# The second product of the feed-forward in float32r parts, and new orders of work in three kinds of attention block

## The reference

```python
x = layernorm(x + differential_attention(x))        # 16 heads, causal, two softmaxes per head
x = layernorm(x + ffn(x))

def _layer(x, ...):                                 # ffn() applies it twice (DEPTH = 2)
    h = shift_token(x)                              # second half of the channels one token later
    q, k, v = split(h @ wqkv, 3)                    # 8 heads of 64
    q, k = rotary_xpos(l2norm(q) * qs, l2norm(k) * ksc)
    x = x + local_attention(q, k, v) @ wo           # window 128, own and previous window
    h = layernorm(shift_token(x)) * lg + lb
    a, g = split(h @ w1 + b1, 2)                    # HID = 682
    x = x + (a * gelu(g)) @ w2 + b2
    return x
```

## Time and profile before

| | |
|---|---|
| median of 3 runs | 5556.42 us (5554.65 to 5564.04) |
| the profiled execution | 5557.89 us, span of its instructions 5555.8 us |
| granted TensorE clock over the span | 0.991 of full speed |
| busy: TensorE, VectorE, ScalarE, GpSimd | 95%, 75%, 63%, 23% |

### The profile page before, as it was taken

One profiled execution on the slowest core, in us unless ns is written; L12 is line 12 of the kernel. 1 busy time (PEld: TensorE's weight loads), 2 busy tenths in 40 slices (PEclk: granted clock), 3 DMA queues, 4 the chain that ended last, 5 costly groups with the idle time before them and its releaser, 6 DMA issues.

```text
span 5555.8 us, 150327 instructions
## 1 busy us (share of the span) xinstructions
PE 5271.0 (95%) x59592; PEld 2996.7 (54%) x59592; DVE 4168.2 (75%) x10819; ACT 3509.1 (63%) x7119; POOL 1259.2 (23%) x2489
## 2 busy tenths in 40 slices
PE   8999999999999999999789999999999999999997
PEld 3444444444444444544356666666666666666664
DVE  6888878888887888878567777777776777777774
ACT  4676667666666766767556566565565656656664
POOL 2222222222222222222212112111122121221211
PEclk9999999999999999999899999999999999999999
DMA  3333333233333333323110000000000000000000
GB/s 71 56 56 66 54 62 61 50 71 56 64 55 54 69 54 69 54 50 68 44 43 12 16 9 16 16 9 16 16 26 26 20 16 20 24 16 20 16 20 20
DMA packets 128829, 216.97 MB, mean 39 GB/s; under 512 B 40064, under 2 KB 40192, under 8 KB 127360
## 3 DMA queue, kind: packets, MB, share of 16 engines
q1 hardware_dynamic: 128128, 207.35, 18.4%
HBM read 46.78 MB, written 25.17 MB: 13 GB/s over the span
## 4 chain that ended last, share of the span: by engine, by line
PE 64%; ACT 15%; DVE 10%; issue 7%; POOL 4%; DMA 0%; POOLq 0%; ACTq 0%; SPq 0%; DVEq 0%
PE ps L617 23%; PE ps L746 14%; PE ps L1108 6%; PE ps L869 4%; ACT pt L1327 3%; PE ps L970 3%; PE ps L951 3%; PE ps L943 2%; ACT sm L1461 2%; DVE sm L1922 2%; ACT gates L1559 1%; PE ps L1049 1%; PE ps L1045 1%; PE ps L1046 1%; PE ps L927 1%
## 5 line engine op out<-in xcount | busy, mean ns | idle before, releaser
L1327 ACT ACTIVATE pt<-ps 128x1024 f32<-128x1024 f32 (+7 forms) x2048 | 1237.4, 654 | 620.1 <-PE ps L617 464.4
L746 PE MATMUL ps<-pt,va 128*32 128x512 f32 (+3 forms) x3072 | 1226.3, 487 | 22.3 <-POOL pt L2224 22.2
L746 PE MATMUL ps<-pt,ones 128*32 128x512 f32 (+3 forms) x6144 | 1236.3, 488 | 0.0
L746 PE MATMUL ps<-pt,vs 128*32 128x512 f32 (+3 forms) x3072 | 1230.0, 488 | 0.0
L1748 DVE CUSTOM_DVE_ANT_0 junk<-ps,causal 128x128 bf16<-128x128 f32 (+3 forms) x2048 | 978.1, 488 | 307.5 <-PE ps L617 291.7
L617 PE MATMUL ps<-kt,qt 96*32 96x512 bf16 (+3 forms) x12288 | 1017.4, 328 | 35.5 <-DVE mc L1748 16.3
L2224 POOL TENSOR_SCALAR_AFFINE_SELECT pt<-pt 128x256 f32<-128x256 f32 x1024 | 465.8, 455 | 1937.8 <-ACT pt L1327 1936.3
L617 PE MATMUL ps<-qt,kt 98*32 98x512 bf16 (+3 forms) x12288 | 836.6, 328 | 22.8 <-ACT pt L1327 22.0
L1752 DVE TENSOR_REDUCE mc<-ps 128x1 f32<-128x512 f32 x1024 | 706.4, 690 | 155.2 <-PE ps L617 124.5
L617 PEld LDWEIGHTS ps<-kt,qt 96*32 96x32 bf16 x12288 | 335.7, 94 | 578.4 <-DVE mc L1752 224.8
L1461 ACT ACTIVATE sm<-sm,mxw 128x256 f32<-128x256 f32 (+1 forms) x1024 | 494.0, 486 | 150.1 <-DVE mxw L1922 149.7
(11 more groups left out here) (170 smaller groups left out, 10221.6 us busy)
## 6 DMA issues: line engine op xcount, KB each, us to landing
qt<-part SPq DMA_DIRECT2D x768, 64.0 KB, 2.4
kt<-part SPq DMA_DIRECT2D x768, 64.0 KB, 2.5
ya<-wy SPq DMA_DIRECT2D x128, 128.0 KB, 2.3
yb<-wy SPq DMA_DIRECT2D x128, 128.0 KB, 2.3
xs<-between_phases SPq DMA_DIRECT2D x32, 512.0 KB, 3.8
xt<-in_x SPq DMA_DIRECT2D x16, 512.0 KB, 6.2
between_phases<-z SPq DMA_DIRECT2D x16, 512.0 KB, 2.8
between_phases<-xo SPq DMA_DIRECT2D x16, 512.0 KB, 2.7
```

What stands on the lines that cost most here:

```text
L746: mmi = pe.matmul(ps[32 * q:32 * q + 32, 4 + half, lo - half * 512:hi - half * 512], w, probs(kb)[:, i, lo - first(kb):hi - first(kb)], st ...
L1327: act.activation(probs(kb)[:, i, kb * P - first(kb):1024 - first(kb)], ps[:, 2 * i:2 * i + 2, :].rearrange("p a q -> p (a q)")[:, kb * P:1 ...
```

## The change

It does seven things, all in the second phase.

1. ffn_out is made in float32r parts: w2 is split once a layer into w2h (ScalarE) and w2l (GpSimd, in the place of w2) at the end of the block W % 64 = 5; the gated product is written over the gates, copied to hhh (inner_high, ScalarE) and the rest subtracted to hhl (inner_low, GpSimd, in the place of the gates). Each float32 matmul becomes three float32r ones, and the first half of the outputs waits for hhl row block by row block.
2. TensorE, c = 0 and c = 3: keys(W + 1) goes ahead of transpose_p(W, 0), and the other transposes stand elsewhere among the products.
3. TensorE, c = 2: scores(W, 2) and (W, 3) go ahead of transpose_p(W, 0), transpose_p(W, 2) and (W, 3) in among the hidden products, weigh behind all of them.
4. ScalarE, c = 2: exps(W, 2), exps(W, 3) and place_p(W, 1) go ahead of the Gelu table and the Gelus; place_p(W, 2) and (W, 3) follow the Gelus, and inner_high(m, 0) to (m, 4) stand in the rest of the block. In c = 0 and c = 3 squares(W + 1) goes ahead, exps(W, 2) and (W, 3) back; inner_high(m, 5) stands in c = 3.
5. VectorE: norms and rotations go forward between the normalises in c = 0 and c = 3; in c = 2 normalise(W, 2) and (W, 3) go between the gated products; final_add goes behind residual, final_normalise behind the gated products.
6. GpSimd: split_x(W + 2) becomes the first step of each block, with a third buffer of xh and xl; sum_channels goes ahead of final_channels; inner_low is added in c = 2 (behind VectorE's combine) and c = 3.
7. gate_out's first step waits for w2_full, since the gates' place is in use until the second product has been made.

```diff
-        xh = sb("xh", [P, 2, 2, P], F32R)
+        xh = sb("xh", [P, 3, 2, P], F32R)
@@ TensorE, ffn_out
-                    pe.wait_ge(w2_ready, sent(m // (2 * nb) + 1))
-                    pe.wait_ge(hh_done, done(m * HB + 6))
+                    pe.wait_ge(w2l_done, done(m // (2 * nb) + 1))
+                    pe.wait_ge(hh_done, done(m * HB + 5))
...
-                    mmi = pe.matmul(ps[:, fbank(m, 19 + oc), :], w2[rows, j, oc * P:(oc + 1) * P], hh[rows, j, :],
-                                    start=j == 0, stop=j == HB - 1)
+                    if oc == 0:
+                        pe.wait_ge(hhl_done, done(m * HB + j + 1))
+                    pe.matmul(out, w2h[rows, j, cols], hhh[rows, j, :], start=j == 0, stop=False)
+                    pe.matmul(out, w2l[rows, j, cols], hhh[rows, j, :], start=False, stop=False)
+                    mmi = pe.matmul(out, w2h[rows, j, cols], hhl[rows, j, :], start=False, stop=j == HB - 1)
@@ TensorE, c == 0 (c == 3 the same)
-                    transpose_p(W, 0)
                     keys(W + 1, 0)
                     keys(W + 1, 1)
+                    transpose_p(W, 0)
                     values(W, 0)
@@ TensorE, c == 2
                     keys(W + 1, 1)
+                    scores(W, 2)
+                    scores(W, 3)
                     final_variance(m - 1, W)
                     transpose_p(W, 0)
                     values(W, 0)
                     values(W, 1)
                     transpose_p(W, 1)
-                    scores(W, 2)
-                    scores(W, 3)
...
+                    hidden(m, 0, True)
+                    hidden(m, 1, True)
+                    hidden(m, 2, True)
                     transpose_p(W, 2)
+                    hidden(m, 3, True)
+                    transpose_p(W, 3)
+                    hidden(m, 4, True)
+                    transpose_q(W + 1)
                     weigh(W, 0)
@@ ScalarE
+            def inner_high(m, j):
...
+                act.wait_ge(hh_done, done(m * HB + j + 1))
+                act.activation(hhh[rows, j, :], gb_[rows, j, :], ACT.Copy).then_inc(hhh_done, 1)
@@ ScalarE, c == 2
                     values(W)
+                    exps(W, 2)
+                    exps(W, 3)
+                    place_p(W, 1)
                     inverse_norms(W + 1)
                     gelu_table(m)
                     gelu(m, 0)
...
                     gelu(m, 5)
-                    exp_table(m)
-                    exps(W, 2)
-                    exps(W, 3)
-                    place_p(W, 1)
                     place_p(W, 2)
                     place_p(W, 3)
+                    exp_table(m)
+                    inner_high(m, 0)
                     place_q(W + 1)
                     place_k(W + 1)
                     heads_high(W)
+                    inner_high(m, 1)
+                    inner_high(m, 2)
+                    inner_high(m, 3)
+                    inner_high(m, 4)
@@ VectorE, c == 3
                     normalise(W, 0)
+                    largest(W, 2)
+                    largest(W, 3)
                     normalise(W, 1)
-                    largest(W, 2)
-                    normalise(W, 2)
-                    largest(W, 3)
                     norms(W + 1)
                     rotate_own(W + 1)
+                    normalise(W, 2)
+                    rotate_other(W + 1)
                     normalise(W, 3)
-                    rotate_other(W + 1)
@@ GpSimd
+            def inner_low(m, j):
...
+                pool.wait_ge(hhh_done, done(m * HB + j + 1))
+                pool.tensor_tensor(hhl[rows, j, :], gb_[rows, j, :], hhh[rows, j, :], ALU.subtract).then_inc(hhl_done, 1)
...
+                split_x(W + 2)
+                if W % 4 == 3:
+                    inner_low(m, 5)
...
+                if m >= 0 and W % 4 == 2:
+                    pool.wait_ge(rot_done, done(W + 2))
+                    for j in range(5):
+                        inner_low(m, j)
```

More of the change, by code:

```diff
@@ L1226, in attend @@
                     ffn_out(m, 0, (2,), True)
-                    transpose_p(W, 1)
+                    transpose_p(W, 2)
                     ffn_out(m, 0, (3,), True)
@@ L1645, in attend @@
                     exps(W, 1)
+                    inner_high(m, 5)
+                    squares(W + 1)
+                    place_p(W, 0)
                     exps(W, 2)
-                    place_p(W, 0)
-                    squares(W + 1)
                     inverse_norms(W + 1)
@@ L1681, in _ @@
             exp_table(m)
+            for j in range(HB):
+                inner_high(m, j)
             final_squares(m)
@@ L2009, in gated @@
                     return
-                if j == 0:
-                    dve.wait_ge(w2_full, done(2 * m))
                 dve.wait_ge(ge_done, done(m * HB + j + 1))
@@ L2042, in attend @@
                     largest(W, 3)
-                    final_add(m - 1)
                     normalise(W, 1)
+                    norms(W + 1)
+                    rotate_own(W + 1)
                     normalise(W, 2)
+                    rotate_other(W + 1)
                     normalise(W, 3)
@@ L2048, in attend @@
                         add_bias(W // (nb * WIN))
-                    norms(W + 1)
-                    rotate_own(W + 1)
-                    rotate_other(W + 1)
                     combine(W + 1)
@@ L2054, in attend @@
                     residual(m, 1)
+                    final_add(m - 1)
                     centre(m)
@@ L2324, in _ @@
                 if m >= 0 and W % 4 == 0:
+                    sum_channels(m)
                     final_channels(m - 1)
-                    sum_channels(m)
                     sum_squares(m)
```

92 lines of the change are left out of this document (51 added, 41 removed).

## The result

The changed kernel takes 5617.35 us (median; 5616.74 to 5622.14) against 5555.53 us for the kernel before in the same comparison (5553.00 to 5564.04): a ratio of 1.011, 95% interval 1.0093 to 1.0128. It is slower by 62 us. The profiled execution has a span of 5615.0 us (before 5555.8) and a mean granted clock of 0.982 (before 0.991).

The account below looks back on a forecast made before the run. TensorE, busy 95% of the span, was taken to set the pace by its own order of work; -5 (c = 3) + 34 (c = 2) + 10 (c = 0) + 5 (once each) + 15 (clock) = +59 on 5557.9, so 5615 us, range 5545 to 5668.

Parts of the forecast that it names:

- c = 0: Blocks of kind 0: +1 us from the new order, +9 us from final_add meeting sum_channels in layer 2.
- c = 3: Second-product blocks: 22.59 us to 22.4, -0.15 a block, -5 us over 31 blocks, ends -25 and +34.
- c = 2: Gelu blocks: the later Gelu chain makes 21.54 us into 22.6, +1.1 a block, +34 us in all (+19 to +50).
- the wait on gated: Sign: in c = 2, hidden's first pass waits for VectorE's gated product about 3 us a block instead of 0.4.
- normalise above 0.69: Sign of meetings on the shared port: VectorE's normalise should take longer than 0.69 us, or GpSimd's subtractions longer than 1.3.
- subtractions above 1.3: Sign of meetings on the shared port: GpSimd's subtractions should take over 1.3 us, or VectorE's normalise over 0.69.
- the granted clock of 0.5: Sign: the clock's 1.2 GHz level should show behind TensorE's stalls in c = 2.
- once-each work: Splitting w2 twice and the tail, where the parts are made with nothing beside them: +5 us together, 0 to +12.
- the clock: Lower clock level behind most c = 2 stalls: +0.5 us a block, +15 us in all, ends 0 and +34.
- rival 1: c = 3 gives its full saving, -65 us; ends at 5541, deciding if c = 3 falls below about 20.9; chance 0.13.
- my price without meetings, 21.7: c = 3 block length without port meetings: 21.7 us, with waits of 0.3 and 0.9 back at two transposes.
- best case of 20.5: c = 3 block at best: 22.59 us falls to 20.5, with 1.75 saved on passes and about 0.34 wait hidden.

Follow-up runs that it names:

- e1: Changed kernel with the c = 2 blocks back in their old order on TensorE, ScalarE and VectorE: 5566.4 us, 1.001 of the kernel before.
- e10: e9 with w2l split in six pieces and layer 2's final_add at its old place in halves with short c = 0 blocks: 5482.9 us.
- e3: Changed kernel with GpSimd's six subtractions per half cut to 16 of 512 columns, TensorE's passes kept: 5573.1 us, 1.002 of the kernel before.
- e6: e5 with the second product's copies and subtractions moved to where VectorE needs no two SBUF inputs: 5508.9 us, 0.9908 of the kernel before.
- e8: Kernel before with only the new c = 0 and c = 3 orders and sum_channels ahead of final_channels, float32 product kept: 5546.5 us, ratio 0.9978.
- e9: e6 with layer 2's final variance between hidden 1 and 2 on TensorE, and final_inverse later on ScalarE: 5494.4 us, 0.9875 of the kernel before.
- e2: Changed kernel without ScalarE's two table loads in c = 2, a plain copy in place of the Gelu: 5539.0 us, 0.996 of the kernel before.
- e5: Changed kernel with ScalarE's c = 2 order altered: exps 2 ahead of values, place_p 1 behind the second Gelu: 5569.6 us, 1.002 of the kernel before.
- e7: e6 with w2l made in six pieces and final_add ahead of normalise 1 in the halves with long c = 0 blocks: 5508.3 us, ratio 0.9909.
- e4: Changed kernel with inner_high 1 to 4 moved into c = 3 and GpSimd's next-layer weight split ahead of inner_low: 5610.4 us, ratio 1.0085.

## Why the prediction was right, and which of its steps were off

The forecast (5615 on the profiled execution's 5557.9) and the measured 5617 agree, and the mechanism that it put first carries the loss: e1 gives 54 of the second phase's 60 us back by c = 2's order alone. Of the signs it named, the wait on gated (0.4 to 3.0 us), normalise above 0.69, subtractions above 1.3 (four took 5.47 us) and the granted clock of 0.5 are all there. The terms, though, agree less well than their sum: that it came within 2 us is luck, as c = 0 and the once-each work miss by 16 and 15 us in opposite directions, and c = 2 and the clock by 18 and 14. Two of the bounds do not follow from the prediction's own figures: the lower end of c = 3 is 31 x 0.89 = 28 us and not 25, and the range starts at 5545, above the 5541 of rival 1 that it says it reaches.

| term | predicted | measured |
|---|---|---|
| c = 2 without the clock, 31 blocks | +34 (19 to 50) | +15.6 in 29 steady blocks |
| the clock | +15 (0 to 34) | +29.1, 19 drops |
| c = 0 | +10 | -6.2 |
| c = 3 | -5 (-25 to +34) | 0 in steady blocks |
| once each | +5 (0 to 12) | +20 |

**c = 2.** The start was right: Gelu at 12.1 said, 11.92 measured; hidden 2 behind it at 13.38 (13.6 said), which is 0.2 of the difference. The end was summed too long: I had combine end at 19.5 and transpose_q wait 0.6 us for it, but normalise with its reciprocal and gated follow one another every 1.46 us, not 1.67, combine ends at 18.64, and transpose_q comes at 18.69 with hardly a wait. So a block with the clock up is +0.48 us in layer 1 and +0.60 in layer 2, not +1.1; the sum, 15.6, is below my lower bound of 19. The bounds varied ScalarE's chain alone; VectorE's, summed from single durations, was the one that was off.

**The clock.** The wait was foreseen, as was that not each one brings the lower level. The price of one was too low: I let part of the 1.6 us be hidden by the wait for combine, which did not exist; each drop costs 1.5 us, in 8 of 15 steady blocks of layer 1 (12.1 us) and 11 of 14 of layer 2 (17.0 us). Two errors that both came, in part, from that 0.6 us wait cancelled within c = 2: +44.7 us against +49.

**c = 0.** The step that failed is the sign. I feared norms' wait for squares in the short blocks (+0.5; measured -0.03) and gave the long ones -0.3 (measured -0.64). That final_add would cost the 7 short blocks of layer 2 by meeting sum_channels was right in kind (+0.54, said +1.3 on top of +0.5), and e10 takes it back; that it would take back the gain of the long ones was wrong (-0.63). The meeting is there in both kinds (sum_channels takes 2.17 us in W = 72 and in W = 76, 1.27 before), but TensorE reaches the mean later in a long block and waits only 0.31 us for it, against 1.18 in a short one.

**c = 3.** 22.61 measured, 22.4 said. The full first meeting (0.94 us, 0.8 said) and the one at the scaling behind the norms are there. But my price without meetings, 21.7, was wrong: e3 has 21.00 and e6 20.76. I had taken ScalarE's copies ahead of the exps as a cost of about 1.0 us (2.3 less 1.48 gives 0.8; the first exp came 0.67 later, at 2.69 against 2.02); keys, moved ahead of the first transpose, covers it, as e3 has the exp at 2.69 too and no wait at the first two transposes. So the meetings cost 1.6 us and the rest, by the best case of 20.5, at most 0.5, where I had 0.7 and 1.2. That best case was itself too low: the passes save 1.63 us (e6 against e8), not 1.75, and keys ahead of the transpose 0.20 (e8), not 0.34; 20.76 is the block without a wait.

Rival 1 (c = 3 gives its full saving) named 20.9 us as the point from which it decides, and the meetings are nearly all that kept the changed kernel from it: e3, without them, has 21.00, and e6 20.76 in layer 1. By the Trainium skill, page "SBUF — State Buffer", section "SBUF: two separate sides", whichever of VectorE (with two inputs from SBUF) and GpSimd (reading SBUF) starts first keeps the shared port pair for the whole instruction. The trace agrees: in the changed kernel normalise 0 started 0.2 us behind a subtraction and lost 0.94 us; in e6 normalise 1 starts 0.99 us behind the last subtraction, near its end, and loses 0.16. In both cases, and for normalise 0 of e6 (0.32 us of the fifth subtraction left, 0.19 lost), the loss is what was left of the subtraction less 0.13 to 0.14 us.

**Once each.** +5 was too little: 6.2 us in the tail, 4.0 at the layer switch (split_wqkv stands behind inner_low on GpSimd, which the prediction did not follow), and 11.0 in the blocks W = 2, 6 and 70, of which the last two hold the splits of w2 and the lower clock as well; -1.3 is the phase's start.

Left open: why the clock fell behind one wait of 3.0 us and not behind the next like it. In layer 1 it is, from the fourth of the steady blocks on, every second one; with the same waits in e3 it fell in 11 of these 15 blocks, not 8. So something besides the wait's length decides, perhaps its place in time; no run here moved the place alone.

## What to carry to other kernels

Where two engines hand buffers to one another through a third, sum the chain from the first late result to the end of the block, on every engine that it passes, and take the pitch of alternating operations from a place where they do alternate. Before a product is split into cheaper passes, ask where the work that makes the parts can run without holding the port of an engine that is on the path: here the same subtractions cost VectorE 1.6 us a block, or 0.6 (0.35 and 0.22, layer 1) in another place. A wait of the busiest engine should be filled with work that is due anyway (e9) or kept short, since the lower clock behind it can add 1.3 to 1.6 us more, behind a wait of 2.0 us as behind one of 3.0.

## What the runs showed of the hardware

- The granted clock by the length of TensorE's wait in c = 2: no drop behind waits of 0.4 us (before, e1), 1.2 us (14 steady ones of layer 2 in e2) or 1.6 us (15 steady ones of layer 1 in e2, as many in e5), a drop behind 7 of 14 of 2.0 to 2.1 us (layer 2 of e5; 6 of 14 in e6, 5 of 14 in e7) and behind 19 of 29 of 2.6 to 3.0 us (changed kernel). Each drop cost 1.3 to 1.6 us of its block there; in six blocks of e3 and two of e4 it lasted longer and cost 2.6 to 2.9.
- An operation on 16 columns can lose as much to GpSimd as a large one: the scaling behind the norms took 0.84 and 1.17 us instead of 0.17. VectorE's operations that read one input from PSUM (gated, 0.75 us in e6; largest, 0.42) and its sum over the norms (1.22 in e4) keep their times beside GpSimd's subtractions.
